# One step of a gated linear attention kernel: who turns k, who normalises x, who stores

## What is computed

```python
x = L0_attn_x                                   # 4 x 2048 x 512, fp32
x = x + attn(layernorm(x), Wq, Wk, Wv, Wo, Wa, ba)
x = x + ffn(layernorm(x), CB, SCB, bias)
# attn: 16 heads of 64
q, k = elu(x @ Wq) + 1, elu(x @ Wk) + 1;  v = x @ Wv
a = sigmoid(x @ Wa + ba + 2.0)                  # one decay a head and token
# for each token t:
S = a[t] * S + k[t] v[t]^T;  z = a[t] * z + k[t]
out[t] = (q[t] @ S) / (q[t] @ z + eps)
return out @ Wo
# ffn: x @ CB^T * (SCB / 127) + bias
```

## Time and profile before

| | us |
|---|---|
| median of 3 runs | 1965.36 |
| lowest, highest | 1963.75, 1965.54 |
| the profiled execution | 1965.75 |
| its span, first to last instruction | 1964.0 |
| TensorE busy in it | 1939.4 |
| VectorE busy | 1645.7 |
| ScalarE busy | 687.1 |
| GpSimd busy | 389.6 |

### The profile page before, as it was taken

How to read it: one execution, slowest core, us unless ns; L and a number is a source line. 1 busy time by engine, 2 the same in 40 slices (tenths; PEclk the granted TensorE clock), 3 DMA queues, 4 the chain that set the end, 5 groups by cost and what they waited for, 6 DMA issues and landing times.

```text
span 1964.0 us, 69099 instructions
## 1 busy us (share of the span) xinstructions
PE 1939.4 (99%) x26926; PEld 1690.8 (86%) x26926; DVE 1645.7 (84%) x2918; ACT 687.1 (35%) x1288; POOL 389.6 (20%) x368
## 2 busy tenths in 40 slices
PE   8999999999999999999999999999989999999999
PEld 7888888898888888988888888888878888888887
DVE  8788888888888888888888888888787777777776
ACT  5334334333433343344333433343422222222221
POOL 3222222232222222332222223222010000000000
PEclk9999999999999999999999999999999999999999
DMA  6343443444443444444344444445476666666665
GB/s 217 89 94 96 99 115 94 110 106 104 100 97 98 105 105 108 104 104 105 97 98 102 108 101 107 105 108 128 98 164 163 161 161 161 161 160 160 161 161 117
DMA packets 596067, 237.40 MB, mean 121 GB/s; under 512 B 432064, under 2 KB 546240, under 8 KB 596032
## 3 DMA queue, kind: packets, MB, share of 16 engines
q1 hardware_dynamic: 560896, 204.94, 43.9%
q10 hardware_dynamic: 35136, 32.00, 5.7%
HBM read 168.59 MB, written 51.97 MB: 112 GB/s over the span
## 4 chain that ended last, share of the span: by engine, by line
PE 95%; DVE 2%; issue 1%; DMA 1%; SPq 1%; POOL 0%; ACT 0%; POOLq 0%; DVEq 0%
PE G L1325 54%; PE DS L1283 17%; PE NUM L1283 9%; PE NUM L1394 4%; PE SC L1447 3%; PE DS L1426 3%; PE NUM L1408 3%; PE SC L1273 2%; PE DS L1467 1%; DVE w_lo L912 0%; DMA attn_cols<-attn 0%; SPq L429 0%; DMA norm_rows<-moments 0%; DMA abc<-decay_rows 0%; DVE D L1109 0%
## 5 line engine op out<-in xcount | busy, mean ns | idle before, releaser
L1325 PE MATMUL G<-w_hi,xT_hi 128*128 128x512 f32 x1024 | 406.9, 397 | 0.4 <-DVE w_lo L912 0.4
L1325 PE MATMUL G<-w_lo,xT_hi 128*128 128x512 f32 x1024 | 399.8, 390 | 0.0
L1325 PE MATMUL G<-w_hi,xT_lo 128*128 128x512 f32 x1024 | 398.7, 389 | 0.0
L734 ACT ACTIVATE relu_t<-G 128x512 f32<-128x512 f32 x256 | 153.4, 599 | 451.9 <-PE G L1325 449.9
L1325 PE MATMUL G<-xT_hi,w_hi 128*128 128x256 f32 x1024 | 290.2, 283 | 0.2 <-DVE w_lo L912 0.2
L1325 PE MATMUL G<-xT_lo,w_hi 128*128 128x256 f32 x1024 | 289.8, 283 | 0.0
L1325 PE MATMUL G<-xT_hi,w_lo 128*128 128x256 f32 x1024 | 289.7, 283 | 0.0
L1325 PEld LDWEIGHTS G<-w_hi,xT_hi 128*128 128x128 f32 x1024 | 192.4, 188 | 42.2 <-issue 0.6
L1325 PEld LDWEIGHTS G<-w_hi,xT_lo 128*128 128x128 f32 x1024 | 192.3, 188 | 41.4
L1325 PEld LDWEIGHTS G<-w_lo,xT_hi 128*128 128x128 f32 x1024 | 192.6, 188 | 35.5
L702 ACT ACTIVATE w_hi<-at_rows 128x512 fp32r<-128x512 f32 x128 | 73.8, 624 | 383.7 <-PE DS L1283 365.9
(11 more groups left out here) (137 smaller groups left out, 3609.0 us busy)
## 6 DMA issues: line engine op xcount, KB each, us to landing
abc<-decay_rows SPq DMA_DIRECT2D x256, 128.0 KB, 3.2
pbc<-product_rows SPq DMA_DIRECT2D x256, 128.0 KB, 3.1
attn_cols<-attn SPq DMA_DIRECT2D x512, 64.0 KB, 2.2
at_rows<-attn_cols ACTq DMA_DIRECT2D x244, 128.0 KB, 2.8
xt<-in_x SPq DMA_DIRECT2D x64, 256.0 KB, 3.1
x_in<-in_x SPq DMA_DIRECT2D x64, 256.0 KB, 3.0
out_rows<-xt SPq DMA_DIRECT2D x64, 256.0 KB, 3.0
xT_in<-in_xT SPq DMA_DIRECT2D x31, 512.0 KB, 4.4
```

What stands on the lines that cost most here:

```text
L734: act.activation(relu_t[buffer][:, :], bank[:, :], ACT.Relu)
L1325: made = nc.tensor.matmul(to, lhs, rhs, start=(n == 0), stop=(n == len(passes) - 1))
```

## The change

1. k of heads 8 to 15 no longer goes through TensorE. VectorE turns it in 32x32 blocks into a new tile `k_turned` (`turned_k1`), and SyncE places it in `kT` with four transfers within SBUF (`place_k`), in the step in which it is made; `scores` of the next step waits for them. TensorE turns only k of heads 0 to 7, and ScalarE copies only those.
2. VectorE normalises the columns of x, with one instruction of 1024 elements for the subtraction and one for the product, in even steps. The numbers of the tokens are stored so that each kind lies side by side (`norm_rows` is 4 x 128), which makes their store one of single numbers. `store_norm` stands behind the wait for `num_ready[0]` and `spread_norm` behind the `abc` transfers.
3. ScalarE makes `vw` of group 1 with eight activations of 65 elements, and `S_part` of group 0 with four.
4. GpSimd issues the stores of the attention outputs.
5. VectorE's `elu_k(1, 0)` stands ahead of the two `qs` products.
6. At the end of the block `normalised(1)` of chunk 63 moves to the tail's step 3, the scaling and splitting of the last weights is interleaved with chunks 0 and 1, and the first product of the tail waits for one weight tile at a time.

```diff
+                def place_k():
+                    sp.wait_ge(scores_ready, one[0])
+                    if exists(i - 1):
+                        wait(sp, kT_loaded, k64[-1])
+                    sp.wait_ge(k_turned_ready, one[0])
+                    for g in range(4):
+                        q = SQ * g
+                        sp.dma_start(kT[:, twos(1), q:q + SQ],
+                                     k_turned[q:q + SQ, :].rearrange("f (b t) -> f b t", t=SQ)).then_inc(kT_loaded, 16)
...
-                    sp.dma_start(norm_rows, moments[:, :, :].rearrange("p s a -> p (s a)")).then_inc(norm_stored, 16)
+                    sp.dma_start(norm_rows.rearrange("m c -> c m"), moments[:, :, :].rearrange("p s a -> p (s a)"),
+                                 allow_slow_non_contiguous=True).then_inc(norm_stored, 16)
...
+                def weighted_v1():
+                    act.wait_ge(v_ready[1], one[0])
+                    act.wait_ge(D_ready[1], one[0])
+                    wait(act, delta_ready[1], one[-1])
+                    for h in range(HH, H):
+                        made = act.activation(vw[:, h, :], v1[1 - b][:, h, :], ACT.Copy, scale=D[:, h, L - 1:L])
+                    made.then_inc(vw_ready[1], 1)
+                def carried_on0():
+                    act.wait_ge(pc_ready, one[0])
+                    act.wait_ge(state_ready[0], one[-1])
+                    for j in range(GH):
+                        made = act.activation(S_part[:, j, :], S[b][:, j, :], ACT.Copy, scale=pc[:, j, 0:1])
+                    made.then_inc(carry_ready[0], 1)
...
+                def turned_k1():
+                    if exists(i - 1):
+                        wait(dve, kT_loaded, k64[-1])
+                    dve.wait_ge(k_ready[1], one[0])
+                    nc.vector.transpose(k_turned[:, :].rearrange("p (x j t) -> p x j t", x=4, t=SQ),
+                                        k[:, U:2 * U].rearrange("p (j f x) -> p x j f", f=SQ, x=4))\
+                        .then_inc(k_turned_ready, 1)
...
+                def centred_columns():
+                    dve.wait_ge(xT_loaded, x16[0])
+                    dve.wait_ge(norm_loaded, x16[0])
+                    nc.vector.tensor_tensor(x_tiles, x_tiles, over_tiles(0), ALU.subtract).then_inc(xT_centred, 1)
+                def normal_columns():
+                    dve.wait_ge(xT_centred, pairs[0])
+                    nc.vector.tensor_tensor(x_tiles, x_tiles, over_tiles(1), ALU.mult).then_inc(xT_normal, 1)
...
-                    for r in (1, 0):
-                        if exists(i - r):
-                            for j in range(GH * r, GH * r + GH):
-                                made = halves_turned([SC[:, 512 * a:512 * a + 512] for a in range(2)], j, k)[1]
-                    made.then_inc(kT_ready, 1)
+                    if exists(i):
+                        for j in range(GH):
+                            made = halves_turned([SC[:, 512 * a:512 * a + 512] for a in range(2)], j, k)[1]
+                        made.then_inc(kT_ready, 1)
...
                 if isinstance(i, int) and i == 2:
-                    pe.wait_ge(wf_lo_ready, KT)
-                if exists(i - 2):
+                    pe.wait_ge(num_copied[1], NC)
+                    pe.wait_ge(fT_lo_ready, 1)
+                    for kt in range(KT):
+                        pe.wait_ge(wf_lo_ready, kt + 1)
+                        made = passes(F[0], (fT_hi[0], fT_lo[0]), (wf_hi, wf_lo), range(kt, kt + 1), KT)
+                    made.then_inc(F_ready, 1)
+                elif exists(i - 2):
```

More of the change, by code:

```diff
@@ L540, in step @@
                     ffn_weights()
-                if exists(i - 2):
-                    store_rows(1, i - 2, one[-2])
+                if gates:
+                    store_decays()
+                if b == 1 and exists(i):
+                    place_k()
+                if gates:
+                    sp.wait_ge(decay_stored, p80[1])
+                    if not exists(i):
+                        sp.wait_ge(w_lo_ready, KT)
+                    spread_decays(0, next_pair, 0)
                 if b == 1 and exists(i):
@@ L832, in step @@
                     q_parts(3)
+                    weighted_v1()
                     if closing:
@@ L1124, in step @@
                 if exists(i - 2) and not ending:
-                    normalised(1)
+                    normalised(1, one[-2], a64[-3])
                 if exists(i - 1):
@@ L1141, in step @@
                     decays()
+                if exists(i) and not second:
+                    elu_k(1, 0)
                 for r in (1, 0):
@@ L1247, in step2 @@
                     residual_deviation(one[0], 1 - b)
-                if isinstance(i, int) and i == 1:
-                    ffn_weights_lo()
+                if opening:
+                    turned_lo(1, 0)
+                    ffn_weights_lo(range(2))
+                if isinstance(i, int) and i == 3:
+                    normalised(1, NC, 64 * (NC - 1))
             steps(dve, step2, 1, NC + 3)
```

187 lines of the change are left out of this document (99 added, 88 removed).

## The result

The changed kernel takes 2301.47 us (median of 6 runs, 2294.40 to 2303.75) where the kernel before takes 1965.69: a ratio of 1.1695, 95% interval 1.1682 to 1.1708. That is 357 us more than the 1944.4 that was forecast, and on the other side of no change. Of the rivals it is none, though its sign is that of B and C.

The account below looks back on a forecast made before the run. TensorE was taken as the bound, busy 1939.4 of 1964.0 us. From 1965.75, transposes took off 16.0, the start 1.6, and the end with vanished kT copies 3.7, giving 1944.4 us; range 1936 to 1966.

Parts of the forecast that it names:

- B: Rival, chance 0.07: GpSimd's stores stretch VectorE's instructions as its arithmetic did; 37 us lost, 1981 us.
- C: Rival, chance 0.08: GpSimd's stores wait for gaps in VectorE's work, 3.1 us each against a 2.7 limit; 2140 us.
- The placement: Loop transfers: kT complete about 10 us before the scores need it, nothing waits; a later single-number store costed at nothing.
- A: Rival, chance 0.13: even step's VectorE list comes late, so k0 is late each pair; about 1955, 1966 or 1978 us.
- the stores on GpSimd: 16 output stores a pair on GpSimd: hidden below 2.7 us each; issue bounds taken from SyncE, 0.57 and 2.25 us.
- The second: SyncE's queue in the loop: eight stores of 0.63 us a step replaced by four, so what stands behind comes earlier.
- Part 1 on TensorE: Eight fewer transposes of k per step: 0.25 us each over 64 chunks, 16.0 us less; upper bound 22.7.
- VectorE's list in even steps: VectorE from k to k0 in even steps: finished at 752.1 to 752.5, slack about 0.7 to 1.1 us, costing nothing.
- ScalarE in even steps: Eight activations before k0's relu: 0.9 to 1.8 us, 3.0 at worst, against 1.66 idle; taken as no cost.
- Rival D: Rival, chance 0.04: TensorE's gaps without a releaser grow by 10 us and kT eats the tail's gain; about 1960 us.
- The start: TensorE's 1.96 us wait for VectorE's k near 47 us: 1.6 us less, bounds 0 and 2.0.
- The end of the block: Last chunk and tail: kT's wait costs 2.1 and 0.5, vanished waits and slow products give 6.1; 3.5 us less.

Follow-up runs that it names:

- e13_pairs_last_store: Changed kernel with spread products ahead of placements in odd steps, norm numbers as 256 pieces of 8 bytes, GpSimd's last store behind weight scaling: 1953.58 us, ratio 0.9941.
- e5_row_and_order: Changed kernel with norm numbers stored as 128 pieces of 16 bytes and, in odd steps, SyncE's spread products ahead of the placements: 1962.05 us, ratio 0.9986.
- e7_stores_by_sp: e5_row_and_order with the 16 stores of attention outputs a pair back in SyncE's queue: 1969.37 us.
- e2_before_singles: Kernel before with only the norm numbers' store changed to single numbers, and the layout that goes with it: 2177.82 us, ratio 1.1092.
- e6_order_alone: Changed kernel with only SyncE's order in odd steps changed, spread products ahead of placements; the store of single numbers stays: 2174.49 us.
- e16_spare_late: e13_pairs_last_store plus an unneeded ScalarE store of 512 single zeros each even step, after the copy of outputs of heads 0 to 7: 2049.30 us.
- e15_spare_early: e13_pairs_last_store plus an unneeded ScalarE store of 512 single zeros each even step, right after the copies of kT: 2125.19 us.

## Why the prediction was wrong

- **The step that failed** is in "The placement": "The store of single numbers may land later than the store of rows did; ... I cost it at nothing, or at the A below." It lands after 10 us instead of 2.2, holds transfers of its own and of other queues meanwhile (`abc` 13.2 us, the spread 8.4), holds SyncE's list at the wait for it, and where it is issued early TensorE stops. It alone costs 213 us in the kernel before, 212 to 258 in the changed one. Why pieces of 4 bytes do this stays open. No row of before showed its price, and it was not bounded from both sides as the stores on GpSimd were; its bound was taken from slack (half a step), not from rows. The rival that the measurement asks for, a transfer of many tiny pieces that is late, was not on the list. A's sign is in the profile, a wait before the transposes that VectorE's k releases, but its last cause is not VectorE's list or ScalarE's exp: it is `abc` and the spread.
- **The second**, the sentence before it: "SyncE's queue loses eight stores ... so what stands behind them comes earlier." On the sum of issues that is right. The order was not followed: in odd steps the placements wait for `k_turned`, and `pbc`, pc and the copy of kT stand behind them. 81 to 127 us. The prediction looked at who waits for kT, not at who is queued behind it.
- **Part 1 on TensorE**, 0.25 us a step, is right to 0.01 (0.26 in the odd step). VectorE's list in even steps, finished by 752.1 to 752.5 with a slack of 0.7 to 1.1, was about right too: with the layout of pairs the even step gained 0.22. With rows, 1.6 us longer, it has no slack, and vw on VectorE costs 24.6 us.
- **ScalarE in even steps**: eight activations take 2.0 us (row mean 342 ns, each about 0.25 us after the other), 0.2 above the upper estimate of 1.8 and inside the bound of 3.0; in the loop of `e13_pairs_last_store` TensorE does not wait for it.
- **Rivals B and C** fell by rows: qT at 0.69 us, a store at 0.62. They carried 0.15 of the chance for the right sign by the wrong mechanism. C was also priced too high: the row of 1.29 us is of two `qs` products, and with one of them the sum is 0.63 + 0.65 + 1.18 = 2.5 us, under C's own limit of 2.7. The Trainium skill's rules behind them ("SBUF — State Buffer") fare apart. "Who interferes with whom" agrees with the vanished stretch. The 3100 ns of a GpSimd transfer in "A bandwidth-pool intuition that's wrong", which are for a `tensor_copy` on VectorE, didn't come up as an issue that long (0.81 us at most); a landing of 3.3 us in `e5_row_and_order` instead of SyncE's 2.2 in `e7_stores_by_sp` is what the rows have.
- **Rival D** falls as well: TensorE's waits without a releaser are 6.8 us in all before, and 7.2 in `e13_pairs_last_store`.
- **The start**: 2.4 us less by `e13_pairs_last_store` (its step 4 begins 3.2 us sooner, 0.8 of it by transposes); 1.6 was said.
- **The end of the block** was to give 3.5 us; in `e13_pairs_last_store`, counted from the last step of the loop, it costs 3.8. The wait for the placed k was forecast at 2.1 and measured at 2.3 (1.1 in `e5_row_and_order`). Not seen were 2.7 us in which `delta` waits for ScalarE's vw in step 63, with the turn of k and D ahead of it, and 2.0 us for the split weights in the tail (1.2 and 0.8). In the changed kernel's own order GpSimd's last store adds 5.4. The sum of terms was made of who no longer waits, without a new look at VectorE's and GpSimd's lists there.

The profiled execution of `e13_pairs_last_store` took 1951.85 us, 7.45 above the forecast. The end of the block, 3.8 + 3.5 = 7.3, is nearly all of that; the other terms are within 1 us of theirs.

## What to carry to other kernels

A store is not priced by its bytes: 2 KB in 512 pieces of 4 bytes took 10 us and held transfers of all queues, its issuer's list and, issued early, TensorE, while 64 KB in 512 pieces of 128 bytes took 2.2. Where a change gives a transfer a new shape, look at the size and the number of its pieces, and give it a price of its own even if slack seems to cover it. Then, for each wait that is put into a queue, write down what stands behind it and who waits for that, one engine further than the tensor that is being moved.

## What the runs showed of the hardware

- A store of 512 single numbers lands after 10 us, as one transfer or as four. 256 pieces of the same 2 KB take 3.9 us in the loop, 128 take 1.4, and 512 pieces of 128 bytes take 2.2.
- While it is under way, the DMA engines of the core move little or nothing (0.13 of their time in 8 us of the changed kernel, 0.00 in 8.7 us of `e2_before_singles`), and transfers issued on other queues land late too (12.2 instead of 5.8 us in `e6_order_alone`, 9.4 instead of 5.8 in `e16_spare_late`).
- Where it is issued early in a step, TensorE's stream stops for some 3 us with no releaser, although nothing it uses is moved. In `e15_spare_early` no engine's work needed the store, and the same bytes as 128 pieces cost nothing clear of noise. What TensorE is short of there is not shown. That it is its instructions fits the word "issue", but the trace gives no sign of it: of the 35 packets of instructions on the page of that run, none lies between 168 and 1531 us, where the stops of the loop are.
- GpSimd stood 3.85 us before the eighth store in a row, with VectorE idle. Groups of four, ten us apart, were issued without such a stop in most steps. Its cause stays open.
- VectorE reads numbers 8 bytes apart as fast as neighbours (1.20 us for 1024 elements) and 16 bytes apart in 1.98 us and more. The Trainium skill, "SBUF — State Buffer", section "Door 1: The DMA port swizzle", in its box on SBUF's cachelines, has lines of 16 bytes and wants at least two hits in one; the rows agree with that. Its "4 fp32" as the distance that is free does not fit them.
